# A gather of pixels on ScalarE, cut into two halves at other places of its order

## The chip, the cores and the metric

The kernel runs on one NeuronCore of a Trainium2 chip. The metric is the time of one execution on the device, in microseconds. TensorE multiplies matrices and writes to PSUM, VectorE, ScalarE and GpSimd work element by element, and SyncE starts the transfers from memory. Each engine has its own queue, is served in order, and waits on semaphores for the others.

## What is computed

128 images of 64 channels and 64 x 64 pixels go through three stages in float32. Cut to what matters:

```python
# token stage: 4 x 4 pixels of an image give one token
reduce_feats = x.mean(over the 16 pixels)                  # 256 tokens x 64 channels
q  = layernorm(reduce_feats) @ Wq.T                        # 8 heads of 8 channels
kv = layernorm(each of the 16 pixels) @ Wkv.T              # 16 keys and values a token
attn = softmax(q * scale . k over the 16 pixels)
h = reduce_feats + (attn . v) @ proj_w.T + proj_b
# linear attention with decay over the 256 tokens, in chunks of 128
scores = (q_c . k_c) * mask;  intra = scores . v_c
inter = (q_c * q_decay) . S;  S = decay * S + (k_c * k_decay) . v_c
h = layernorm(h + (intra + inter) @ w_proj + b_proj)
# eight experts, the best two for each token, weighted
h = layernorm(h + h + sum_e combine[:, e] * (gelu(h @ w1[e] + b1[e]) @ w2[e] + b2[e]))
```

(The last line has h twice, since the expert block itself returns its tokens plus the sum.)

## The kernel before

The kernel has two blocks, one behind the other. The first runs the token stage and the attention, the second the experts. The change is in the first.

**Units.** A unit is one half (128 tokens, 2048 pixels) of two images. Their 2 x 64 channels fill the 128 partitions, each with 2048 pixels in a row. There are 128 units. Every engine runs the same function `step(i, r)` for unit 4 i + r, in a loop whose body holds four units, and in each step it works at several units at once: `there(i, r, lag)` says whether the unit `lag` back exists, `done(i, r, lag, per)` gives the count that a semaphore has when that unit is done, if it is raised `per` times a unit. The order of the operations inside a step is written out by hand, for each engine apart. `s` is the unit's parity, which is also the half of the images.

**The pixels.** `xb` holds four units of pixels as they come from memory. In a row of 2048 pixels the 16 pixels of a token are four neighbours (`d`) in each of four blocks (`b`). The value product on TensorE wants them with the tokens side by side, so ScalarE copies each fourth pixel of `xb` into `xd`: `gather(j, ahead)` (L590 on, the copy at L597) brings piece d = j, all four blocks, 512 elements a partition. Pieces 0 and 1 are gathered for the next unit (`ahead` = 1) in the step before, pieces 2 and 3 in the unit's own step. Each raises `xd_done` once, four times a unit.

**ScalarE's order in a step.** gather(2); `ssb` (L606, a copy of the selected sums); gather(3); attention's queries and keys `qT`, `kT` (L615, L616), which are ready when TensorE's L447 is; squares for a layer norm (L572); `vpad` (L626), in every second unit the state copies `vpl`, `kpl` (L632, L633), and `htok` (L634), all out of TensorE's L457; centred(0) (L579); more squares; the reciprocal deviations by logarithm and exponential (L648 to L651, the last being `y0s`); centred(1); values(0) (L586, a copy of the first values); `oT` (L657); centred(2); `aggT`; gather(0) and later gather(1) of the next unit; values(1); `qqT` (L668); the exponential of the softmax (L672); centred(3).

**TensorE's order.** selected sums (L355, L359); scores of the attention (L472); its queries and keys (L446, L447); a transposition of `ssb` (L370); attention's values, keys and tokens (L457); keys 0 (L389, L394: the key product and the centred pixels for `b` = 0); queries (L431); values of pieces 0 and 1 (L416); part of attention's sums (L491); keys 1; the rest of L491; keys 2; a transposition (L507); values of pieces 2 and 3 (L416); another transposition (L440); keys 3; projections (L512, L520), and every second unit the state (L527). L457 writes the bank out of which `kT` is copied, so it waits for `qk_ev`. Ahead of it in the queue stand the waits for keys 0 (`keys_free(0)`): the pixels of the unit, the first half of the mask, and the previous unit's readers of the same banks. `values_free(v)` holds back the value products: it waits for the pieces in `xd`, by the count of `xd_done`.

**VectorE's order.** the mask (L883, two instructions, PSUM to `sm`); keys 0 (L872: key product times query, out of PSUM); the reduce of the weighted values (L894); keys 1 (L872); a Newton step on the reciprocal deviations (L901 to L903); queries; keys 2; softmax's maxima (L927 to L932); keys 3; the attention weights `aw` (L939); the token `hT` (L951) and the attention's output (L964).

**GpSimd's order.** weights times values (L711, four instructions into `pv`) as soon as `aw` is there; two sums over them (L718); `qm` (L725), `htok` (L731), `kd` or `qdm`; and the sums of the pixels (L765 to L772) for the tokens of a later unit.

Of the kernel before, what the change touches and what calls it, by code (L numbers as in the profile page):

```python
# [13 lines left out]
def vit_tower_kernel(nc, x, ln_q_w, ln_q_b, Wq, ln_kv_w, ln_kv_b, Wkv, proj_w, proj_b,  # L14
# [3 lines left out]
    ST = 4  # L18
# [18 lines left out]
    def done(i, r, lag, per, plus=0):  # L37

        if isinstance(i, int):
            return max(0, max(0, min(UNITS, 4 * i + r - lag + 1)) * per + plus)  # L40
        return i * (4 * per) + (r - lag + 1) * per + plus

    def there(i, r, lag):
        return not isinstance(i, int) or 0 <= 4 * i + r - lag < UNITS

    def pairs(i, r, back, per=1):

        if isinstance(i, int):
            return max(0, min(UNITS // 2, 2 * i + r // 2 + back)) * per
        return i * (2 * per) + (r // 2 + back) * per  # L50
# [32 lines left out]
    with ExitStack() as ctx:  # L83
# [3 lines left out]
        def sem(name):  # L87
            return ctx.enter_context(nc.semaphore(name))
# [47 lines left out]
        with ExitStack() as early:  # L136
            def sb1(name, shape, dt=F32):
                return early.enter_context(nc.sbuf_tensor(name, shape, dt))
# [19 lines left out]
            xb = sb1("xb", [P, 4, PX])  # L158
            xt = sb1("xt", [P, PX // 2])
            xd = sb1("xd", [P, ST, PX // ST])  # L160
# [50 lines left out]
            xd_done = sem("xd_done")  # L211
# [56 lines left out]
            def heads(ap):  # L268
                return ap.rearrange("p (m c) -> p m c", c=C)
# [57 lines left out]
            def _(pe):  # L327
# [16 lines left out]
                def step(i, r):  # L344
# [54 lines left out]
                    def values_free(v):  # L399

                        if there(i, r, 0):
                            pe.wait_ge(mask_done, done(i, r, 4, NM))
                            pe.wait_ge(vs_done, done(i, r, 1, NV, v))
                            pe.wait_ge(xd_done, done(i, r, 1, ST, 2 * v + 2))

                    def values(v):

# [127 lines left out]
                    attn_vk()  # L535
                    keys(0)
                    values_free(0)
                    queries()
                    values(0)
                    attend(0)  # L540
                    keys(1)
                    attend(1)
                    keys(2)
                    values_free(1)
                    aggregated()
                    values(1)
# [9 lines left out]
            def _(act):  # L556
# [9 lines left out]
                def step(i, r):  # L566
# [3 lines left out]
                    def squares(src, dst, to=None):  # L570

                        return nc.scalar.activation(src if to is None else to, src, ACT.Square, accum_out=dst)  # L572

                    def centred(j):

                        if there(i, r, 0):
                            act.wait_ge(kc_pe, done(i, r, 1, ST, j + 1))
                            act.wait_ge(sel_pe, done(i, r, 1, 1))
                            nc.scalar.activation(sqs[:, j, :], CB, ACT.Square).then_inc(cs_done, 1)  # L579

                    def values(v):

                        if there(i, r, 0):
                            act.wait_ge(v_pe, done(i, r, 1, NV, v + 1))
                            act.wait_ge(pv_ch, done(i, r, 2, ST, 2 * v + 2 - ST))
                            nc.scalar.activation(  # L586
                                vs[:, s, v * 8 * P:(v + 1) * 8 * P].rearrange("p (n m c) -> p m n c", m=2, c=C),
                                ps[:, 2:4, :].rearrange("p m (n c) -> p m n c", c=C), ACT.Copy).then_inc(vs_done, 1)

                    def gather(j, ahead):  # L590

                        if there(i, r, -ahead):
                            f = (r + ahead) % 4
                            if j == 0:
                                act.wait_ge(x_in[f], 16 * NL * (i + 1 + (r + ahead) // 4))
                            act.wait_ge(v_pe, done(i, r, 1 - ahead, NV, j // 2 + 1 - NV))
                            nc.scalar.activation(  # L597
                                xd[:, j, :].rearrange("p (b t) -> p b t", b=ST),
                                xb[:, f, :].rearrange("p (b t d) -> p d b t", b=ST, d=ST)[:, j],
                                ACT.Copy).then_inc(xd_done, 1)  # L600

                    gather(2, 0)
                    if there(i, r, 1):
                        act.wait_ge(sel_pe, done(i, r, 1, 1))
                        act.wait_ge(tr_pe, done(i, r, 2, 1))
                        nc.scalar.activation(ssb[:], B7, ACT.Copy).then_inc(sev_done, 1)  # L606
                    gather(3, 0)
                    if there(i, r, 3):
                        act.wait_ge(qk_pe, done(i, r, 3, 1))
                        act.wait_ge(sc_done, done(i, r, 5, 4))  # L610
# [6 lines left out]
                    if there(i, r, 5):  # L617

                        act.wait_ge(lt_done, done(i, r, 5, 1))
                        for m in range(2):  # L620
                            ins = squares(LT[:, m * CR:m * CR + C], ssq[:, m:m + 1], l2[:, m * C:(m + 1) * C])
                        ins.then_inc(ln_sq, 1)
                    if there(i, r, 3):
                        act.wait_ge(vk_pe, done(i, r, 3, 1))
                        act.wait_ge(lt_done, done(i, r, 5, 1))
                        nc.scalar.activation(  # L626
                            vpad[:, o, :].rearrange("p (m h w) -> p m h w", m=2, w=VW)[:, :, :, 0:D],
                            B67[:, :, 0:C].rearrange("p m (h d) -> p m h d", d=D), ACT.Copy).then_inc(vk_ev, 1)
                        if s == 1:
                            act.wait_ge(s_pe, pairs(i, r, -1))  # L630
                            act.wait_ge(kd_done, pairs(i, r, -1))
                            nc.scalar.activation(heads(vpl[:]), B67[:, :, 0:C], ACT.Copy).then_inc(st_ev, 1)  # L632
                            nc.scalar.activation(heads(kpl[:]), B67[:, :, C:2 * C], ACT.Copy).then_inc(st_ev, 1)  # L633
                        nc.scalar.activation(htok[:, o, :].rearrange("p (m c) -> p m c", c=CR),  # L634
                                             B67[:, :, 2 * C:2 * C + CR], ACT.Copy).then_inc(vk_ev, 1)
# [13 lines left out]
                    link(nc.scalar.activation(lnv[:], sgr[:, :, 16:19], ACT.Ln, bias=eps_c[:, 0:1], scale=1.0 / C))  # L649
                    link(nc.scalar.activation(y0[:], lnv[:], ACT.Exp, scale=-0.5))  # L650
                    nc.scalar.activation(y0s[:], y0[:], ACT.Square).then_inc(rs_ch, 1)  # L651
                    centred(1)
                    values(0)
                    if there(i, r, 4):
# [4 lines left out]
                    if there(i, r, 2):  # L659
                        act.wait_ge(agT_pe, done(i, r, 2, 1))  # L660
                        act.wait_ge(pj_done, done(i, r, 3, 1))
                        nc.scalar.activation(aggT[:], B6[:, 0:P], ACT.Identity, bias=bv_col[:, 0:1],
                                             scale=N / WS).then_inc(agT_ev, 1)
                    gather(0, 1)
                    values(1)
                    if there(i, r, -1):
# [7 lines left out]
                    centred(3)  # L674
                    gather(1, 1)
                units(act, step)

            @block.gpsimd
# [743 lines left out]
```

## Time and profile before

| | us |
|---|---|
| median of three runs | 2465.64 |
| lowest, highest | 2463.54, 2467.04 |
| profiled execution | 2467.91 |
| its span | 2466.0 |

| engine | busy us | share of the span | instructions |
|---|---|---|---|
| TensorE, matmuls | 2225.0 | 90% | 32433 |
| TensorE, weight loads | 1025.5 | 42% | 32433 |
| VectorE | 1830.5 | 74% | 4000 |
| ScalarE | 1844.4 | 75% | 4405 |
| GpSimd | 1883.8 | 76% | 2077 |

The span is the time from the first to the last record of one execution, taken by the hardware profiler. Busy times are sums over records; records of one engine can overlap by a little, as an instruction starts before the last one's end is recorded. PE is TensorE, PEld its weight loads, DVE VectorE, ACT ScalarE, POOL GpSimd, SP SyncE; L12 is line 12 of the kernel.

### The profile page before, as it was taken

How to read it: one execution, taken by the hardware profiler on the slowest of the kernel's cores; microseconds unless marked ns; L12 is line 12 of the kernel's file. 1: busy time of each engine (PE TensorE's matmuls, PEld its weight loads, DVE VectorE, ACT ScalarE, POOL GpSimd, SP SyncE). 2: the span in 40 equal slices, each digit the busy share in tenths (PEclk: the TensorE clock that was granted, in tenths of full speed). 3: DMA queues.
4: the chain of work that ended last, by engine and by line, in shares of the span. 5: the costliest groups of instructions: out<-in, count | busy, mean ns of one | idle time of the engine just before them, and what ended most of it. 6: DMA issues, size and time to landing. Idle time of an engine off the chain costs nothing. (4 is left out here: it accounts for less than half of the span.)

```text
span 2466.0 us, 90547 instructions
## 1 busy us (share of the span) xinstructions
PE 2225.0 (90%) x32433; PEld 1025.5 (42%) x32433; DVE 1830.5 (74%) x4000; ACT 1844.4 (75%) x4405; POOL 1883.8 (76%) x2077
## 2 busy tenths in 40 slices
PE   1799999999999999999999999999999976999997
PEld 0344444444444444444444444444444442332222
DVE  4577777777777777777777777777777766777775
ACT  1888888888888888888888888888888854555554
POOL 2788889888889989888898888888888951333333
PEclk9999999999999999999999999999999987999999
DMA  4333333333333333333333333333333200110001
GB/s 83 71 71 70 70 71 73 72 73 72 72 73 71 70 70 70 70 70 70 70 70 70 70 70 70 70 70 70 71 73 73 47 2 1 24 23 21 20 22 28
DMA packets 573782, 147.91 MB, mean 60 GB/s; under 512 B 573504, under 2 KB 573504, under 8 KB 573504
## 3 DMA queue, kind: packets, MB, share of 16 engines
q1 hardware_dynamic: 573504, 143.53, 29.1%
q8 instruction: 256, 4.19, 0.7%
q14 instruction: 22, 0.18, 0.0%
HBM read 135.10 MB, written 8.39 MB: 58 GB/s over the span
## 5 line engine op out<-in xcount | busy, mean ns | idle before, releaser
L711 POOL TENSOR_TENSOR pv<-vs,aw 128x512 f32<-128x512 f32 x512 | 535.7, 1079 | 172.5 <-DVE aw L939 172.5
L597 ACT ACTIVATE xd<-xb 128x512 f32<-128x512 f32 x512 | 589.2, 1186 | 0.0
L389 PE MATMUL ps<-xb,w_ckv 64*64 64x512 f32 x2048 | 551.4, 615 | 5.4 <-DVE kqs L872 4.3
L394 PE MATMUL ps<-xb,w_ckv 64*64 64x512 f32 x2048 | 551.4, 615 | 0.0
L872 DVE TENSOR_TENSOR kqs<-ps,qqT 128x512 f32<-128x512 f32 x512 | 353.8, 691 | 231.1 <-PE ps L394 221.3
L579 ACT ACTIVATE sqs<-ps 128x512 f32<-128x512 f32 x512 | 308.5, 603 | 239.7 <-PE ps L394 239.5
L883 DVE TENSOR_TENSOR sm<-ps,decay 128x1024 f32<-128x1024 f32 x256 | 301.5, 1219 | 149.8 <-PE ps L472 149.8
L765 POOL TENSOR_TENSOR xt<-xb 128x512 f32<-128x512 f32 x256 | 326.2, 1275 | 23.2 <-issue 22.7
L718 POOL TENSOR_TENSOR pv<-pv 128x512 f32<-128x512 f32 x256 | 320.3, 1273 | 0.0
L416 PE MATMUL ps<-w_ckv,xd 64*64 64x64 f32 x16384 | 297.8, 221 | 0.0
L416 PEld LDWEIGHTS ps<-w_ckv,xd 64*64 64x64 f32 x16384 | 262.9, 135 | 33.9 <-issue 1.8
L894 DVE TENSOR_REDUCE agg<-pv 128x128 f32<-128x1024 f32 x128 | 253.5, 1981 | 24.4 <-POOL pv L718 18.9
L586 ACT ACTIVATE vs<-ps 128x1024 f32<-128x1024 f32 x256 | 261.9, 1023 | 0.5 <-PE ps L416 0.5
L1241 ACT ACTIVATE hid<-ps,b1p 128x1024 f32<-128x1024 f32 x128 | 142.7, 1115 | 131.8 <-PE ps L1154 131.7
L1358 DVE TENSOR_TENSOR hid<-ps,hid 128x512 f32<-128x512 f32 x256 | 162.9, 685 | 87.3 <-PE ps L1166 77.7
L491 PE MATMUL ps<-sm,vpad 128*32 128x128 f32 x4096 | 192.0, 284 | 34.6 <-DVE kqs L872 30.4
L768 POOL TENSOR_TENSOR xt<-xt 128x512 f32<-128x512 f32 x128 | 163.9, 1281 | 10.0
L491 PEld LDWEIGHTS ps<-sm,vpad 128*32 128x32 f32 x4096 | 90.6, 109 | 179.7 <-issue 106.8
L1086 POOL TENSOR_TENSOR outb<-y,yrs 128x512 f32<-128x512 f32 x32 | 33.4, 1043 | 154.3 <-DVE yrs L1378 154.3
L472 PE MATMUL ps<-qm,kT 32*128 32x512 f32 x1024 | 148.8, 651 | 0.0
L457 PE MATMUL ps<-w_av,hT 64*128 64x200 f32 x512 | 78.4, 376 | 77.1 <-ACT kT L616 76.7
L355 PE MATMUL ps<-kqs,selk 128*32 128x512 f32 x1024 | 136.4, 605 | 11.7 <-DVE kqs L872 2.7
(227 smaller groups left out, 4145.5 us busy)
## 6 DMA issues: line engine op xcount, KB each, us to landing
xb<-in_x_dram SPq DMA_DIRECT2D x512, 256.0 KB, 4.3
out_dram<-outb SPq DMA_DIRECT2D x128, 64.0 KB, 1.6
w1p<-in_L_ffn_w_dram SPq DMA_DIRECT2D x16, 16.0 KB
w2p<-in_L_ffn_w_dram SPq DMA_DIRECT2D x8, 16.0 KB
b1p<-in_L_ffn_b_dram SPq DMA_DIRECT2D x8, 0.2 KB
b2v<-in_L_ffn_b_dram SPq DMA_DIRECT2D x8, 2.0 KB
sm<-in_L_tok_Wkv_dram SPq DMA_DIRECT2D x4, 16.0 KB, 2.0
w_av<-in_L_attn_w_qkv_dram SPq DMA_DIRECT2D x4, 16.0 KB, 2.1
```

The source lines that it names most:

```text
L389: nc.tensor.matmul(KB[own, :], w_ckv[own, 2 * P + m * C:2 * P + (m + 1) * C], xv[own, j], start=True, stop=True)
L394: mm = nc.tensor.matmul(CB[(1 - m) * C:(2 - m) * C, :], w_ckv[own, m * C:(m + 1) * C], xv[own, j], start=True, stop=True)
L416: mm = nc.tensor.matmul(VB[m][h * C:(h + 1) * C, n * C:(n + 1) * C], xv[own, d, b, h * C:(h + 1) * C], w_ckv[own, P + m * C:P + (m + 1) * ...
L491: mm = nc.tensor.matmul(B5[g * W:(g + 1) * W, 0:P], vpad[:, s, at:at + W], sm[:, (4 * g + jj) * P:(4 * g + jj + 1) * P], start=(jj == 0), ...
L579: nc.scalar.activation(sqs[:, j, :], CB, ACT.Square).then_inc(cs_done, 1)
L586: nc.scalar.activation(vs[:, s, v * 8 * P:(v + 1) * 8 * P].rearrange("p (n m c) -> p m n c", m=2, c=C), ps[:, 2:4, :].rearrange("p m (n c) ...
L597: nc.scalar.activation(xd[:, j, :].rearrange("p (b t) -> p b t", b=ST), xb[:, f, :].rearrange("p (b t d) -> p d b t", b=ST, d=ST)[:, j], A ...
L711: nc.gpsimd.tensor_tensor(pv[:, at].rearrange("p (k d) -> p k d", d=D), vs[:, s, at].rearrange("p (k d) -> p k d", d=D), aw[:, j * W4:(j + ...
L718: nc.gpsimd.tensor_tensor(pv[:, j * 4 * P:(j + 1) * 4 * P], pv[:, j * 4 * P:(j + 1) * 4 * P], pv[:, (j + 2) * 4 * P:(j + 3) * 4 * P], ALU. ...
L765: ins = nc.gpsimd.tensor_tensor(xt[:, h * H:(h + 1) * H], xb[:, f, h * H:(h + 1) * H], xb[:, f, (h + 2) * H:(h + 3) * H], ALU.add)
L872: V.tensor_tensor(kqs[:, j, :].rearrange("p (t d) -> p t d", d=ST), KB.rearrange("p (t d) -> p t d", d=ST), qqT[:, s, :].unsqueeze(2).to_b ...
L883: V.tensor_tensor(sm[:, f * 1024:(f + 1) * 1024].rearrange("p (h c) -> p h c", c=P), ps[:, 2 * f:2 * f + 2, :].rearrange("p g (h c) -> p ( ...
```

## The change

The gather of the fourth piece, gather(3), stood between `ssb` and `qT`. It is done in two instructions of two blocks each (256 elements a partition): the first stands behind the squares and ahead of `vpad`, the second behind `y0s` and ahead of centred(1). `xd_done` now rises five times a unit, and the counts for which TensorE waits follow: 5 per unit, 2 for the first value product, 5 for the second.

```diff
@@ TensorE
-                            pe.wait_ge(xd_done, done(i, r, 1, ST, 2 * v + 2))
+                            pe.wait_ge(xd_done, done(i, r, 1, ST + 1, 3 * v + 2))
@@ ScalarE
-                    def gather(j, ahead):
+                    def gather(j, ahead, b0=0, b1=ST):
                             nc.scalar.activation(
-                                xd[:, j, :].rearrange("p (b t) -> p b t", b=ST),
-                                xb[:, f, :].rearrange("p (b t d) -> p d b t", b=ST, d=ST)[:, j],
+                                xd[:, j, :].rearrange("p (b t) -> p b t", b=ST)[:, b0:b1],
+                                xb[:, f, :].rearrange("p (b t d) -> p d b t", b=ST, d=ST)[:, j, b0:b1],
                                 ACT.Copy).then_inc(xd_done, 1)
@@
                         nc.scalar.activation(ssb[:], B7, ACT.Copy).then_inc(sev_done, 1)
-                    gather(3, 0)
                     if there(i, r, 3):
@@
                         ins.then_inc(ln_sq, 1)
+                    gather(3, 0, 0, ST // 2)
                     if there(i, r, 3):
                         act.wait_ge(vk_pe, done(i, r, 3, 1))
@@
                     nc.scalar.activation(y0s[:], y0[:], ACT.Square).then_inc(rs_ch, 1)
+                    gather(3, 0, ST // 2, ST)
                     centred(1)
```

## Rows read from the trace of the kernel before

**Rows 1.** The page, part 1: busy us (share of the span) xinstructions.

```profile
PE 2225.0 (90%) x32433; PEld 1025.5 (42%) x32433; DVE 1830.5 (74%) x4000; ACT 1844.4 (75%) x4405; POOL 1883.8 (76%) x2077
```

**Rows 2.** Busy time by stretch: stretch, length, PE, PEld, DVE, ACT, POOL, clock, DMA.

```profile
60.00:2025.00 1965.00, 1824.08 (x30623) 896.13 (x30619) 1491.00 (x3129) 1612.25 (x4079) 1736.38 (x1903) 1.00 0.34 68
```

**Rows 3.** The line L939 alone: durations in ns, first and last start in us.

```profile
L939 DVE TENSOR_TENSOR aw<-ps,yrs x128: 414/425/426, 80.7 to 2011.6; 128x256 f32<-128x256 f32 x128
```

**Rows 4.** The waits: who waited for whom, us in total, times, longest.

```profile
PE ps L457 <- ACT kT L616: 76.7, 126, 0.9
...
DVE agg L894 <- POOL pv L718: 18.9, 82, 2.6
```

**Rows 5.** Timeline of ScalarE: start, duration, instruction, [idle before it, what ended it].

```profile
1027.80 1.20 ACT L597 ACTIVATE xd<-xb 128x512 f32<-128x512 f32 x1
1028.87 0.30 ACT L615 ACTIVATE qT<-ps 128x128 f32<-128x128 f32 x1
1029.03 0.31 ACT L616 ACTIVATE kT<-ps 128x128 f32<-128x128 f32 x1
...
1029.49 0.26 ACT L572 ACTIVATION_READ_ACCUMULATOR l<-ps 128x1 f32 x1
1030.23 0.28 ACT L626 ACTIVATE vpad<-ps 128x128 f32<-128x128 f32 x1 [0.49 <-PE ps L457]
...
1033.19 0.24 ACT L651 ACTIVATE y0s<-y 128x48 f32<-128x48 f32 x1
1034.18 0.60 ACT L579 ACTIVATE sqs<-ps 128x512 f32<-128x512 f32 x1 [0.75 <-PE ps L394]
```

**Rows 6.** Timeline of TensorE, the same unit and the one before it.

```profile
1015.80 0.50 PE L431 MATMUL ps<-w_qc,h 64*128 64x136 f32 x4
...
1028.14 0.39 PE L447 MATMUL ps<-hT,w_ak 128*128 128x128 f32 x2
...
1029.59 0.61 PE L457 MATMUL ps<-w_av,hT 64*128 64x200 f32 x4 [0.58 <-ACT kT L616]
```

**Rows 7.** Timeline of GpSimd: the two sums, in two units that follow each other.

```profile
1014.10 2.50 POOL L718 TENSOR_TENSOR pv<-pv 128x512 f32<-128x512 f32 x2
...
1029.70 2.50 POOL L718 TENSOR_TENSOR pv<-pv 128x512 f32<-128x512 f32 x2
```

**Rows 8.** Timeline of VectorE in the unit of rows 5.

```profile
1027.94 2.36 DVE L883 TENSOR_TENSOR sm<-ps,decay 128x1024 f32<-128x1024 f32 x2 [1.30 <-PE ps L472]
...
1032.32 1.96 DVE L894 TENSOR_REDUCE agg<-pv 128x128 f32<-128x1024 f32 x1 [0.19 <-POOL pv L718]
1034.21 0.67 DVE L872 TENSOR_TENSOR kqs<-ps,qqT 128x512 f32<-128x512 f32 x1
```

**Rows 9.** Timeline of VectorE in the two units before that.

```profile
1001.69 1.98 DVE L894 TENSOR_REDUCE agg<-pv 128x128 f32<-128x1024 f32 x1
1003.75 0.69 DVE L872 TENSOR_TENSOR kqs<-ps,qqT 128x512 f32<-128x512 f32 x1
...
1016.64 2.00 DVE L894 TENSOR_REDUCE agg<-pv 128x128 f32<-128x1024 f32 x1
1018.84 0.69 DVE L872 TENSOR_TENSOR kqs<-ps,qqT 128x512 f32<-128x512 f32 x1 [0.20 <-PE ps L394]
```

**Rows 10.** Timeline of TensorE near the end of the first stage.

```profile
2002.88 0.39 PE L447 MATMUL ps<-hT,w_ak 128*128 128x128 f32 x2
...
2003.80 0.61 PE L457 MATMUL ps<-w_av,hT 64*128 64x200 f32 x4
```

**Rows 11.** Timeline of ScalarE at the same place.

```profile
2003.31 0.28 ACT L615 ACTIVATE qT<-ps 128x128 f32<-128x128 f32 x1 [1.08 <-PE ps L447]
2003.48 0.27 ACT L616 ACTIVATE kT<-ps 128x128 f32<-128x128 f32 x1
```

**Rows 12.** Timeline of ScalarE in a unit with the state copies.

```profile
1015.24 0.31 ACT L634 ACTIVATE htok<-ps 128x144 f32<-128x144 f32 x1
```

**Rows 13.** Groups of instructions by form: line, operation, count, busy us, mean ns, idle before.

```profile
L597 ACT ACTIVATE xd<-xb 128x512 f32<-128x512 f32 x512 | 589.2, 1186 | 0.0
```

## The prediction

> **What bounds the kernel now.** I read the page first: TensorE is busy for nine tenths of the span [rows 1]. Then the stretches: 1965 of the 2466 us are the first stage (tokens, queries, attention), at full granted clock, and the change lies wholly in it [rows 2]. Its 128 units come at one pace: the product that makes the attention weights (L939) starts first at 80.7 and last at 2011.6 us, so (2011.6 - 80.7) / 127 = 15.20 us a unit [rows 3]. A change is worth what it takes off those 15.20 us.
>
> A busy engine does not say which wait closes the loop, so the waits come next. TensorE stops once in each unit, at L457 (attention's values, keys and tokens), for ScalarE's copy of the keys: 76.7 us in 126 stops, 0.61 us each [rows 4]. And VectorE's reduce of the weighted values (L894) waits for GpSimd in 82 units. These are two different loops through the same unit, and the forecast hangs on how close the second is to the first.
>
> *Loop B, over TensorE.* In the unit shown, ScalarE runs the gather of the fourth piece from 1027.80; only then come qT at 1028.87 and kT at 1029.03, ending at 1029.34 [rows 5]. TensorE's key product L447 had ended at 1028.14 + 0.39 = 1028.53. L457 starts at 1029.59, 0.25 us after kT's end [rows 6]. Behind it stand in order the first key product, the queries, the values, and the second key product, which VectorE multiplies at 1034.21 (L872).
>
> *Loop A, over GpSimd.* aw -> four products and two sums on GpSimd, the last ending at 1029.70 + 2.50 = 1032.20 [rows 7] -> L894 at 1032.32 -> L872 on the second key product at 1034.21, 1.89 us after L894's start, with no idle time before it [rows 8] -> the third and fourth keys -> the next aw. This loop holds no instruction that the change touches.
>
> Which loop ends last at that L872 is read from its distance to L894. Where GpSimd's loop binds it is 1.89. In a neighbouring unit it is 1003.75 - 1001.69 = 2.06, and in the one between 1018.84 - 1016.64 = 2.20, there with 0.20 us of idle time that TensorE's L394 ends [rows 9]. The pattern follows the loop of four units: two of four read 2.2, one 2.06, one 1.89, and it repeats through the stage. So loop A could close earlier than now by 0.31, 0.17, 0.31 and 0 us: 0.79 over four units, 0.20 a unit.
>
> **The change, part by part.**
>
> *Taken away ahead of qT.* One gather, start to next start 1028.87 - 1027.80 = 1.07 us. qT then waits for L447 instead. At the stage's end, where no gather runs, the trace shows that case: L447 ends at 2002.88 + 0.39 = 2003.27 and qT starts 0.04 later [rows 10, 11]. So qT would start at 1028.57, 0.30 us earlier, not 1.07: ScalarE would idle for the rest. kT ends at 1029.04.
>
> *What is late next at L457.* Its queue of waits has also the first half of the mask (L883 writes sm out of the banks that the keys need): two instructions from 1027.94 for 2.36 us, so the first ends near 1029.13 [rows 8]. The bounds of the lag behind it are 0.05 us (kT's end 2003.75 to L457 at 2003.80) [rows 10, 11] and the 0.25 us of now. L457 therefore goes to between 1029.29 (kT plus 0.25) and 1029.38 (mask plus 0.25): 0.21 to 0.30 us earlier. I take 0.28, as the lag of a wait that is met early is nearer to 0.05.
>
> *First half of the gather, ahead of vpad.* It stands behind the squares, whose last record starts at 1029.49, so after the shift at 1029.19, and begins about 0.14 later (ScalarE records overlap by that much: 1.20 of duration against 1.07 of spacing) [rows 5]. Price: half of 1.07 plus half of the fixed part. The fixed part is at least nothing and at most the 0.16 us that a 128-element copy takes in all (1028.87 to 1029.03), so 0.54 to 0.62 us; as an outer bound the whole 1.07. Vpad can start at 1029.33 + 0.54 to 0.62 = 1029.87 to 1029.95. It needs L457, which then ends at 1029.59 + 0.61 - 0.28 = 1029.92. So it is covered by the 0.49 us of idle time now ahead of vpad, with next to nothing over. Queued behind it are vpad, in every second unit the two state copies, and htok; TensorE's queries (L431) wait for these, at 1015.80 after htok's end at 1015.24 + 0.31 = 1015.55 [rows 6, 12].
>
> *Second half, ahead of centred(1).* Behind y0s at 1033.19 ScalarE idles 0.75 us for TensorE [rows 5]. Shifted with loop B by 0.28, a half from about 1033.06 frees ScalarE at 1033.60 to 1033.68, and the second square is due at 1034.18 - 0.28 = 1033.90. Nothing is charged. VectorE's reciprocal chain waits for y0s, which is ahead of it. TensorE's second value pass, the reader of the fourth piece, comes over 2 us later; its count of five gathers a unit instead of four adds no wait, and the first pass asks for the two pieces gathered in the unit before, as now. Nothing is issued to the DMA queues by it.
>
> A whole gather of 512 elements takes 1186 ns in the mean [rows 13]. The Trainium skill, VectorE: DVE Perf Modes, "The TRN2 errata", says that ScalarE operations with a source in SBUF pay a fixed latency in every instruction, 224 cycles at 1.2 GHz, so that cutting one in two is a loss of 0.19 us a unit; charged in full on the path this would be 24 us over the stage and undo the gain. No row here prices a half, but both halves stand in idle time (0.49 and 0.75 us), so by this rule too the sum stays as it is. The Trainium skill, Advanced Engine Details and Errata, "SBUF Cachelines", charges an access for every new 16-byte line; this gather takes one float of each, which would make its cost go with the elements and a half cost half.
>
> **The sum.** Per unit the gain is the smaller of B's 0.28 and A's room: 0.28, 0.17, 0.28, 0, together 0.73 in four units, 0.18 a unit, and 22.6 us over 124 units in steady state. One thing takes from it: where GpSimd truly binds, L894 starts 0.12 us after the last sum (1032.20 to 1032.32), in the other kinds 0.04 (1014.10 + 2.50 to 1016.64) [rows 7 to 9]. If these take on the 0.08 that lie between, the four units gain 0.23, 0.09, 0.23 and 0, and 5.6 us go; I let about half of it go: 20 us. Profiled execution: 2467.9 (span 2466.0 and 1.9 around it) - 20 = 2447.9. It lies 2.3 us above the median of the three runs, so the forecast for the median is 2465.6 - 20 = 2445.6 us; its own range, with 0.21 to 0.30 at L457 (18 to 24 us) and all or none of the 0.08, is 2442 to 2453.
>
> **The rivals.**
>
> *Both loops shorten (2431 us).* If loop A's 1.89 us is not a floor, every unit gains 0.28: 34.7 us. Against it: GpSimd's durations and the reduce are not touched.
>
> *The second half disturbs the reduce (2454 us).* ScalarE would read SBUF while L894 reads it, from 1033.06 on, which it doesn't now. With 0.1 us more on L894 the rooms are 0.21, 0.07, 0.21 and -0.1: 0.39 in four, 12 us. No row shows such an overlap with a reduce.
>
> *L457 gets no earlier (2464 us, no change).* The change would then move qT and nothing behind it: were the mask or another of the waits already as late as kT, nothing but scheduling noise would be left. For it: the stop at L457 ends 0.25 us after kT, five times the 0.05 us of the stage's end. Against: several waits stand in that queue, and the difference fits their being worked off one by one.
>
> *A half costs like a whole (2476 us, slower).* One place: ahead of vpad. The half would end at 1029.33 + 1.07 = 1030.40, 0.17 us after vpad's start now (1030.23). In every second unit, where the state copies follow, L431 waits 0.25 us behind htok [rows 6, 12], and TensorE is 0.17 us later than now: 64 x 0.17 = 11 us more. It decides from a half of 0.90 us on.
>
> **How the numbers follow.** Forecast 0.57; reduce disturbed 0.10; both loops 0.08; no earlier 0.12; half like whole 0.13. Anything within 0.2% (4.9 us) can't be told from no change here. Faster: 0.57 + 0.10 + 0.08, less 0.02 for the edge, 0.73; same 0.14; slower 0.13. For the range 0.08 (both loops) is left out below and most of the slower rival above: 2434 to 2466.
>
> **What the profile of the changed kernel would show.** qT 0.04 us behind L447 with idle time ahead of it; the stop at L457 cut from 0.61 to about 0.33 us; halves of 0.6 to 0.75 us each, starting 0.5 to 0.6 us before their successor can; idle time ahead of vpad near nothing and ahead of the second square 0.2 to 0.3; L894's wait for GpSimd in nearly all units and more in sum; 1.9 us from L894 to the next L872 nearly everywhere; the pace of L939 at about 15.04 us. Wrong it would be by a half of over 0.9 us, a longer L894, or an L457 that stays put.

## The result, and the profile after

The changed kernel takes 2450.2 us (median, 2448.9 to 2452.2) against 2466.3 for the kernel before (2463.5 to 2467.9) in the same runs: a ratio of 0.9934 with a 95% interval of 0.9919 to 0.9948. The gain is 16.1 us where 20 were forecast; the time is 4.6 us above the forecast of 2445.6 and inside its range of 2434 to 2466. The profiled execution took 2449.9 us with a span of 2448.0, 18.0 less than before.

The page's part 1, the stretch of the first stage and the line of the attention weights (now L940; the lines behind the edit have moved by one) answer to [rows 1 to 3]. Their columns are the same.

```profile
PE 2225.4 (91%) x32433; PEld 1025.9 (42%) x32433; DVE 1825.7 (75%) x4000; ACT 1859.5 (76%) x4533; POOL 1884.4 (77%) x2077
```

```profile
60.00:2010.00 1950.00, 1826.33 (x30625) 897.64 (x30623) 1488.19 (x3131) 1627.70 (x4212) 1737.14 (x1904) 1.00 0.34 69
```

```profile
L940 DVE TENSOR_TENSOR aw<-ps,yrs x128: 414/424/426, 80.6 to 1994.4; 128x256 f32<-128x256 f32 x128
```

ScalarE has 128 instructions and 15 us of work more, TensorE's granted clock is the same 1.00 in this stage, and the kernel is faster. The pace is (1994.4 - 80.6) / 127 = 15.07 us a unit, 0.13 less than before [rows 3], and 127 of these are 17 of the 18 us. So all but about 1 us of the gain is made in the loop of the first stage, as the forecast had it.

The waits say what closes the loop now (engine, line, waited for: us in total, times, longest), to be read against [rows 4]:

```profile
ACT qT L614 <- PE ps L447: 103.8, 127, 4.5
...
DVE agg L895 <- POOL pv L719: 47.4, 127, 2.6
...
PE ps L457 <- ACT kT L615: 30.4, 60, 0.6
PE ps L457 <- DVE sm L884: 23.2, 66, 0.5
...
ACT vpad L626 <- PE ps L457: 2.1, 5, 0.7
```

TensorE's stop at L457 fell from 76.7 to 53.6 us, and 66 of its 126 stops are now put down to the mask. VectorE's wait for GpSimd rose from 18.9 us in 82 units to 47.4 in 127. ScalarE's idle time ahead of vpad is gone, since the first half fills it; in the kernel before it was:

```profile
ACT vpad L626 <- PE ps L457: 63.6, 128, 0.9
```

Timelines of the changed kernel show the mechanism and the part of it that was not foreseen. First ScalarE's, with four units that follow each other, in the numbering of the table below the units 1, 2, 3 and 0 of the round (start, duration, instruction, idle time before it and what ended it):

```profile
1005.48 0.28 ACT L614 ACTIVATE qT<-ps 128x128 f32<-128x128 f32 x1 [0.60 <-PE ps L447]
...
1006.21 0.70 ACT L597 ACTIVATE xd<-xb 128x256 f32<-128x256 f32 x1
1006.84 0.28 ACT L626 ACTIVATE vpad<-ps 128x128 f32<-128x128 f32 x1
...
1020.98 0.28 ACT L614 ACTIVATE qT<-ps 128x128 f32<-128x128 f32 x1 [0.90 <-PE ps L447]
...
1035.82 0.28 ACT L614 ACTIVATE qT<-ps 128x128 f32<-128x128 f32 x1 [0.76 <-PE ps L447]
...
1051.18 0.28 ACT L614 ACTIVATE qT<-ps 128x128 f32<-128x128 f32 x1 [0.81 <-PE ps L447]
```

Then TensorE's in the same four units:

```profile
1005.06 0.39 PE L447 MATMUL ps<-hT,w_ak 128*128 128x128 f32 x2
1006.19 0.61 PE L457 MATMUL ps<-w_av,hT 64*128 64x200 f32 x4 [0.27 <-DVE sm L884]
...
1020.27 0.39 PE L447 MATMUL ps<-hT,w_ak 128*128 128x128 f32 x2
1021.67 0.61 PE L457 MATMUL ps<-w_av,hT 64*128 64x200 f32 x4 [0.54 <-ACT kT L615]
...
1035.24 0.39 PE L447 MATMUL ps<-hT,w_ak 128*128 128x128 f32 x2
1036.52 0.61 PE L457 MATMUL ps<-w_av,hT 64*128 64x200 f32 x4 [0.41 <-DVE sm L884]
...
1050.55 0.39 PE L447 MATMUL ps<-hT,w_ak 128*128 128x128 f32 x2
1051.88 0.61 PE L457 MATMUL ps<-w_av,hT 64*128 64x200 f32 x4 [0.47 <-ACT kT L615]
```

From L447's end to qT's start it is 0.03 us (1005.06 + 0.39 to 1005.48), then 0.32, 0.19 and 0.24. The key product is there in all four units; what differs is the queue of waits ahead of qT. The source writes them in the same order for every unit, but the compiled program does not keep it. The records of the waits themselves, which the grouped views leave out, have the key product's first and three or four others behind it in units 0, 2 and 3; in unit 1 the others stand ahead of it, done by 1003.9, and the key product's is the last. L457 follows: its stop is 0.27 us in the unit with the short lag and 0.54 in the one with the long lag, where next to nothing is left of the gain (0.58 in [rows 6]).

The mask's first half, by which L457 also waits, takes 1.22 us of the 2.36 (VectorE, in units 1 and 3):

```profile
1004.87 2.36 DVE L884 TENSOR_TENSOR sm<-ps,decay 128x1024 f32<-128x1024 f32 x2 [1.09 <-PE ps L472]
...
1035.05 2.35 DVE L884 TENSOR_TENSOR sm<-ps,decay 128x1024 f32<-128x1024 f32 x2 [0.90 <-PE ps L472]
```

In unit 1 it ends at 1006.09, 0.10 us ahead of L457, and kT 0.26 ahead. In unit 3 it ends at 1036.27 together with kT, so this view's choice between the two says little; L457 starts 0.25 us behind kT's end there, as it does in units 0 and 2 and in the kernel before.

VectorE's timeline shows the other loop closing (units 1, 2 and 3), L895 to the second L873, to be read against [rows 8, 9]:

```profile
1009.08 1.99 DVE L895 TENSOR_REDUCE agg<-pv 128x128 f32<-128x1024 f32 x1 [0.50 <-POOL pv L719]
1010.98 0.68 DVE L873 TENSOR_TENSOR kqs<-ps,qqT 128x512 f32<-128x512 f32 x1
...
1024.44 2.01 DVE L895 TENSOR_REDUCE agg<-pv 128x128 f32<-128x1024 f32 x1 [0.22 <-POOL pv L719]
1026.37 0.68 DVE L873 TENSOR_TENSOR kqs<-ps,qqT 128x512 f32<-128x512 f32 x1
...
1039.26 1.98 DVE L895 TENSOR_REDUCE agg<-pv 128x128 f32<-128x1024 f32 x1 [0.35 <-POOL pv L719]
1041.25 0.69 DVE L873 TENSOR_TENSOR kqs<-ps,qqT 128x512 f32<-128x512 f32 x1
```

1.90, 1.93 and 1.99 us, where before the same kinds of unit had 2.20, 1.89 and 2.19 (the table has the last). GpSimd's loop now closes three of the four units. In the fourth, unit 3, the table has 2.08 against 1.92 in the others, so 0.16 us of room is left there.

To compare kernels unit by unit, a table was made from each trace: for the units 24 to 103 (20 rounds of the loop), sorted by their place in the round, the mean distance between two starts of `aw`, the median lag from L447 to qT, and the median distance from the reduce to the key product behind it. Unit 0 is the kind read as 2.06 in the forecast, unit 1 the 2.20, unit 2 the 1.89, unit 3 the second of those at 2.2. Differences given in the text are taken before rounding.

| kernel | distance of `aw`, units 0 to 3 | mean | L447 to qT | reduce to key product |
|---|---|---|---|---|
| before | 14.95, 15.52, 15.06, 15.44 | 15.243 | 0.34 to 0.36 in all | 2.05, 2.20, 1.90, 2.19 |
| after | 14.82, 15.23, 15.07, 15.28 | 15.101 | 0.25, 0.04, 0.32, 0.19 | 1.92, 1.92, 1.92, 2.08 |
| e1, one wait ahead of qT | 14.79, 15.24, 15.07, 15.16 | 15.068 | 0.04 in all | 1.90, 1.93, 1.93, 1.93 |
| e2, GpSimd's waits | 14.82, 15.19, 14.98, 15.26 | 15.063 | as after | 2.00, 1.95, 2.08, 1.99 |
| e5, all waits | 14.73, 15.14, 14.82, 15.14 | 14.957 | 0.04 in all | 1.93, 1.91, 1.91, 1.92 |

### The profile page after: what moved, and what is told of

Read it like the earlier page. It is cut to its first block and busy times, and to the rows that moved or that the text cites. A ratio compares the mean times of both kernels' runs of the same rounds, so it can differ in the third digit from the quotient of the medians.

```text
span 2448.0 us, 90675 instructions
## 1 busy us (share of the span) xinstructions
PE 2225.4 (91%) x32433; PEld 1025.9 (42%) x32433; DVE 1825.7 (75%) x4000; ACT 1859.5 (76%) x4533; POOL 1884.4 (77%) x2077
## 5 line engine op out<-in xcount | busy, mean ns | idle before, releaser
L597 ACT ACTIVATE xd<-xb 128x512 f32<-128x512 f32 (+1 forms) x640 | 608.8, 979 | 0.0
L873 DVE TENSOR_TENSOR kqs<-ps,qqT 128x512 f32<-128x512 f32 x512 | 353.3, 690 | 195.4 <-PE ps L394 185.7
L895 DVE TENSOR_REDUCE agg<-pv 128x128 f32<-128x1024 f32 x128 | 255.3, 1994 | 47.5 <-POOL pv L719 47.4
L1155 PE MATMUL ps<-tokT,w1p 64*128 64x512 f32 x512 | 145.9, 648 | 0.0
```

Source lines behind the costliest of these rows:

```text
L597: nc.scalar.activation(xd[:, j, :].rearrange("p (b t) -> p b t", b=ST)[:, b0:b1], xb[:, f, :].rearrange("p (b t d) -> p d b t", b=ST, d=ST ...
L873: V.tensor_tensor(kqs[:, j, :].rearrange("p (t d) -> p t d", d=ST), KB.rearrange("p (t d) -> p t d", d=ST), qqT[:, s, :].unsqueeze(2).to_b ...
```

## The experiments

The theory (1) is that two loops run through every unit, TensorE's over L457 and GpSimd's over the weighted values, and the later one closes it; the change shortened the first by up to 0.3 us until the second stood in the way, and gave away some of that to the waits ahead of qT. The rivals are (2) that TensorE's loop alone sets the pace, and (3) that what was short of the forecast is the price of the two halves.

**e1: one wait ahead of qT.** This is the changed kernel without the other waits ahead of qT (four, in every second unit three), which earlier waits of the same engine already make sure of.

```diff
                         act.wait_ge(qk_pe, done(i, r, 3, 1))
-                        act.wait_ge(sc_done, done(i, r, 5, 4))
-                        act.wait_ge(qm_done, done(i, r, 5, 1))
-                        act.wait_ge(o_done, done(i, r, 5, 1))
-                        if s == 0:
-                            act.wait_ge(qd_done, pairs(i, r, -2))
```

> The changed kernel, but qT waits for the key product alone; the four other waits ahead of it say what earlier waits of the same queue have already made sure of. Two loops alternate (theory 1: TensorE's over L457, GpSimd's over the weighted values): qT starts 0.04 us behind L447 in all four units of the loop (now 0.04, 0.19, 0.25 and 0.32), L457 comes up to 0.25 us earlier, but GpSimd's loop closes in three of four units, so only about 5 us are gained: 2445 us. Theory 2 (TensorE's loop alone sets the pace): 0.16 us a unit, 20 us: 2430 us. Theory 3 (what was short of the forecast is the price of the halves on ScalarE): no gain, 2450 us.

Measured: 2448.6 us (2447.5 to 2449.2), ratio 0.9925 (0.9912 to 0.9939). Against the changed kernel's 2450.2 the medians differ by 1.6 us and the intervals overlap; in the table the pace falls by 0.033 us a unit, and from the first to the last `aw` it is 3.0 us less (81.3 to 1992.2 us). That is less than the 5 us of theory 1, and by the medians alone it could be nothing, as theory 3 has it; it is e4 that decides on theory 3. Its two timelines, ScalarE and TensorE, in one unit and the next:

```profile
1004.97 0.28 ACT L609 ACTIVATE qT<-ps 128x128 f32<-128x128 f32 x1 [0.62 <-PE ps L447]
...
1020.18 0.28 ACT L609 ACTIVATE qT<-ps 128x128 f32<-128x128 f32 x1 [0.60 <-PE ps L447]
```

```profile
1004.54 0.39 PE L447 MATMUL ps<-hT,w_ak 128*128 128x128 f32 x2
1005.67 0.61 PE L457 MATMUL ps<-w_av,hT 64*128 64x200 f32 x4 [0.27 <-DVE sm L879]
1019.75 0.39 PE L447 MATMUL ps<-hT,w_ak 128*128 128x128 f32 x2
1020.88 0.61 PE L457 MATMUL ps<-w_av,hT 64*128 64x200 f32 x4 [0.27 <-DVE sm L879]
```

The lag is 0.04 us in every unit and L457's stop 0.27 in all of them, so the lags of 0.19 to 0.32 were those waits and nothing else. L457 comes 0.16 to 0.26 us earlier behind L447 in three of four units, and yet only unit 3 got much faster, by 0.13 (unit 0 by 0.03): it was the one with 2.08 us between reduce and key product. Theory 2 wanted 20 us.

**e2: GpSimd's loop shortened.** This is the changed kernel, where on GpSimd and VectorE the wait that is met last stands alone.

```diff
@@ GpSimd
-                        pool.wait_ge(aw_done, done(i, r, 2, 1))
-                        pool.wait_ge(agg_ch, done(i, r, 3, 1))
-                        pool.wait_ge(vs_done, done(i, r, 2, NV))
+                        if not there(i, r, -1):
+                            pool.wait_ge(vs_done, done(i, r, 2, NV))
+                        pool.wait_ge(aw_done, done(i, r, 2, 1))
@@ GpSimd, ahead of the last instruction of the step before
+                        pool.wait_ge(vs_done, done(i, r, 1, NV))
                         pool.wait_ge(qp_pe, done(i, r, -1, 1))
@@ VectorE
                         dve.wait_ge(pv_done, done(i, r, 2, 2))
-                        dve.wait_ge(agg_done, done(i, r, 3, 1))
```

> The changed kernel, but GpSimd's first product waits for the attention weights alone (its other waits moved ahead of the instruction before, or dropped as already made sure of), and VectorE's reduce for the sums alone. GpSimd's loop gets 0.08 to 0.17 us shorter. Theory 1 (two loops alternate): the units in which it closes the loop gain up to the distance to TensorE's, 0.1, 0.06, 0 and 0 us of four, about 5 us: 2445 us. Theory 2 (TensorE's loop alone): no change, 2450 us. A theory in which GpSimd's loop alone sets the pace: 0.13 us a unit, 16 us: 2434 us.

Measured: 2445.1 us (2443.5 to 2447.0), ratio 0.9913 (0.9900 to 0.9927), as theory 1 had it in sum: 0.15 us in four units against 0.16. Its spread was another: 0.01, 0.04, 0.08 and 0.02 us in units 0 to 3, where two units were to have 0.1 and 0.06 and the others nothing. More than half of the gain is in unit 2, the unit that gained nothing by the change itself. The weights' product and GpSimd's first product in two units, VectorE first:

```profile
1000.72 0.42 DVE L940 TENSOR_TENSOR aw<-ps,yrs 128x256 f32<-128x256 f32 x1
1015.89 0.42 DVE L940 TENSOR_TENSOR aw<-ps,yrs 128x256 f32<-128x256 f32 x1
```

```profile
1001.22 4.18 POOL L712 TENSOR_TENSOR pv<-vs,aw 128x512 f32<-128x512 f32 x4 [0.63 <-DVE aw L940]
1016.40 4.19 POOL L712 TENSOR_TENSOR pv<-vs,aw 128x512 f32<-128x512 f32 x4 [1.04 <-DVE aw L940]
```

It is 0.50 us from the start of the one to that of the other in all units (0.50 to 0.67 before and after, by the place in the round). So GpSimd's loop does set the pace in some units of the changed kernel: theory 2 alone falls.

**e3: the whole gather ahead of vpad.** In the changed kernel both halves become one instruction at the place of the first, and TensorE counts four gathers a unit, as before.

```diff
-                    gather(3, 0, 0, ST // 2)
+                    gather(3, 0)
@@
-                    gather(3, 0, ST // 2, ST)
```

> The changed kernel, but the whole fourth gather stands ahead of vpad. This is the place of the slower rival: vpad 0.45 us later than in the changed kernel, htok too, and the queries on TensorE 0.43 us later in every second unit and 0.24 us in the others, 0.27 us a unit after the slack of the loop: 2483 us. If the place ahead of vpad is not on the path: 2450 us.

Measured: 2479.0 us (2478.3 to 2482.1), ratio 1.0053 (1.0037 to 1.0068): slower than before the change. ScalarE and then TensorE, in a unit with the state copies:

```profile
1020.78 1.18 ACT L597 ACTIVATE xd<-xb 128x512 f32<-128x512 f32 x1
1021.84 0.30 ACT L626 ACTIVATE vpad<-ps 128x128 f32<-128x128 f32 x1
```

```profile
1022.90 0.50 PE L431 MATMUL ps<-w_qc,h 64*128 64x136 f32 x4 [0.47 <-ACT htok L634]
```

The queries stop for `htok`, as the slower rival said they would, and the time is near the 2476 us that it gave. In the mean of its units vpad starts 0.45 us behind L457's end instead of 0.04. So the rival's mechanism is real; what did not hold is its condition, a half that costs like a whole.

**e4: no fourth gather.** It is left out of the changed kernel, and the piece stays zero (one memset more in the set-up); TensorE counts three gathers a unit.

```diff
+                link(V.memset(xd[:], 0.0))
@@
-                    gather(3, 0, 0, ST // 2)
@@
-                    gather(3, 0, ST // 2, ST)
```

> The changed kernel without the gather of the fourth piece: it is left out, the piece is zero throughout. Theories 1 and 2 (the halves lie in idle time): 2449 us, as the changed kernel. Theory 3 (the halves are paid for on the path, in ScalarE's time or in the reduce that runs beside the second): 2440 us or less.

Measured: 2453.8 us (2452.1 to 2454.7), ratio 0.9946 (0.9931 to 0.9962). Not faster than the changed kernel, but 3.6 us slower; of these 2.8 are the memset: the first `aw` starts at 83.3 instead of 80.6 us. The pace by the table's method is 15.095 us against 15.101. So the halves cost about 0.006 us a unit, under 1 us together, and theory 3 falls. What can be seen of them is in the reduce, in the groups of e4 first and of the changed kernel second (mean ns behind the busy time):

```profile
L894 DVE TENSOR_REDUCE agg<-pv 128x128 f32<-128x1024 f32 x128 | 253.1, 1978 | 47.8 <-POOL pv L717 47.6
```

```profile
L895 DVE TENSOR_REDUCE agg<-pv 128x128 f32<-128x1024 f32 x128 | 255.3, 1994 | 47.5 <-POOL pv L719 47.4
```

**e5: all waits.** e1 and e2 together, and on TensorE:

```diff
@@ keys_free
                             if j == 0:
-                                pe.wait_ge(x_in[r], 16 * NL * (i + 1))
                                 pe.wait_ge(mask_done, done(i, r, 4, NM, 1 - NM))
+                                return
@@ attn_vk
                             pe.wait_ge(qk_ev, done(i, r, 3, 2))
-                            pe.wait_ge(sev_done, done(i, r, 1, 1))
@@ ahead of attn_qk()
+                    if there(i, r, 0):
+                        pe.wait_ge(x_in[r], 16 * NL * (i + 1))
```

> The changed kernel with the edits of e1 and e2 together, and on TensorE L457 waits for the copies and the mask alone (the pixels' wait moved ahead of the attention's queries, the others dropped as already made sure of). Theory 1 (two loops alternate): the reduce-to-key-product distances of e2 (2.00, 1.95, 2.08, 1.99 us) leave 0.08, 0.03, 0.16 and 0.07 us to GpSimd's floor of 1.92, 0.085 a unit, 10 us below e2: 2435 us, with 1.9 us in all four units. Theory 2 (TensorE's loop alone): its own gain is 0.19 us a unit, 24 us: 2421 us.

Measured: 2433.4 us (2432.4 to 2434.6), ratio 0.9867 (0.9852 to 0.9882): 12 us below e2 and 17 below the changed kernel, the fastest of all. The edits of e1 and e2 gave 1.6 and 5.1 us alone; together with the third they give 16.8, which is what two loops in turn do: each edit alone runs into the other loop. The third edit, on TensorE, was not run alone, nor the first two without it. It takes 0.05 us off the stop at L457 (0.27 to 0.22), and if all of that were gained in every unit it would be 6 us; the 11 that are left are still more than the sum of 6.7. The waits of e5:

```profile
DVE agg L891 <- POOL pv L715: 61.8, 127, 2.7
...
PE ps L456 <- DVE sm L881: 27.9, 124, 0.3
```

TensorE stops 0.22 us at this place, in nearly all units for the mask; the reduce is followed by the key product at 1.91 to 1.93 us in all four units, GpSimd's floor.

**e6: the kernel before with e2's edit.** The first lines of it:

```diff
@@ GpSimd
-                        pool.wait_ge(aw_done, done(i, r, 2, 1))
-                        pool.wait_ge(agg_ch, done(i, r, 3, 1))
-                        pool.wait_ge(vs_done, done(i, r, 2, NV))
+                        pool.wait_ge(aw_done, done(i, r, 2, 1))
...
@@ VectorE
-                        dve.wait_ge(agg_done, done(i, r, 3, 1))
```

> The kernel before with e2's edit alone. Theory 1: GpSimd closes the loop there in one unit of four, by 0.03 us: 1 us, 2465 us, no change. If GpSimd's loop sets the pace of the kernel before as well: 0.13 us a unit, 16 us, 2450 us.

Measured: 2463.7 us (2462.9 to 2467.6), ratio 0.9995 (0.9986 to 1.0004): no change. Before the change GpSimd's loop had room in three of four units, and shortening it gave nothing. In the fourth, unit 2, the two loops end together: with the edit the distance from reduce to key product rises from 1.90 to 2.13 us, and the unit gets no faster (15.05 us against 15.06). Behind the change the same edit gave 5 us.

**e7: the whole gather ahead of centred(1).** In the changed kernel both halves become one instruction at the place of the second, with four gathers a unit again.

```diff
-                    gather(3, 0, 0, ST // 2)
@@
-                    gather(3, 0, ST // 2, ST)
+                    gather(3, 0)
```

> The changed kernel, but the whole fourth gather stands ahead of centred(1), behind the reciprocal deviations. It takes 1.07 us of an idle stretch of 0.75: the second square is 0.14 to 0.23 us late and holds TensorE by 0.03 to 0.1 us a unit: 2458 us. If the squares have slack enough: 2450 us, and cutting the gather in two was not needed.

Measured: 2467.7 us (2465.2 to 2469.7), ratio 1.0006 (0.9996 to 1.0015). The expectation had the place right and the price too small by 10 us. ScalarE, then TensorE:

```profile
1003.69 1.17 ACT L597 ACTIVATE xd<-xb 128x512 f32<-128x512 f32 x1
1004.75 0.59 ACT L579 ACTIVATE sqs<-ps 128x512 f32<-128x512 f32 x1
```

```profile
1005.49 0.42 PE L491 MATMUL ps<-sm,vpad 128*32 128x128 f32 x8 [0.44 <-ACT sqs L579]
```

The second square comes right behind the gather and ends at 1005.34; TensorE stops for it 0.44 us, where it stopped 0.24 for VectorE in the changed kernel. From the key product to the next `aw` it is 0.09 to 0.19 us more than in the changed kernel. This stretch belongs to both loops, so nothing absorbs a delay in it. The whole gather fits neither of the two places; that is why the cut pays.

**e8: the kernel before with e1's edit.** The same waits are dropped, in the kernel before.

```diff
                         act.wait_ge(qk_pe, done(i, r, 3, 1))
-                        act.wait_ge(sc_done, done(i, r, 5, 4))
-                        act.wait_ge(qm_done, done(i, r, 5, 1))
-                        act.wait_ge(o_done, done(i, r, 5, 1))
-                        if s == 0:
-                            act.wait_ge(qd_done, pairs(i, r, -2))
```

> The kernel before with e1's edit alone: qT waits for the key product alone. Theory 1: the queue of waits lies under the fourth gather there, so nothing changes: 2466 us. If the waits cost time of ScalarE wherever they stand: 5 us or more less.

Measured: 2467.0 us (2463.4 to 2469.8), ratio 1.0001 (0.9992 to 1.0011): nothing. The lag from L447 to qT stays at 0.34 to 0.35 us in all units. The same queue of waits was there before, but was worked off while the fourth gather ran. The change took this cover away.

## Why the prediction was right, and where it was off

*What bounds the kernel*: right. Loop B over L457 and loop A over GpSimd are what e1, e2, e5 and e6 show, and the floor of 1.89 us between reduce and key product holds: no kind of unit is below 1.90 in any run of the table, and those that GpSimd's loop closes have 1.90 to 1.93.

*qT earlier by 0.30 us*: right for one unit of four. The trace of the stage's end, on which the 0.04 us rested [rows 10, 11], shows a unit whose other waits stand ahead of the key product's in the compiled program and were done 1.5 us before it. In three units of the loop the key product's wait stands first, and the others, though met, are worked off behind it. So the step failed for the units 0, 2 and 3, with 0.25, 0.32 and 0.19 us. The prediction named such waits, worked off one by one, for L457 and did not ask for them at qT. The gains by unit show it: forecast 0.17, 0.28, 0 and 0.28, measured 0.12, 0.29, -0.01 and 0.16 (the table's first two rows). That is 0.57 us a round instead of 0.73, or 17.7 instead of 22.6 us over 31 rounds, and 3.7 of the 4.9 us that are short are unit 3's, the one in which TensorE's loop is the later. The rest is mostly unit 0's, where the room was 0.13 (2.05 to the 1.92 of now) and not 0.17.

*The mask as next at L457*: right in unit 1, and in e1 in 124 units, at 0.27 us against the 0.33 forecast. L457 is then 0.10 us behind the mask's first half, not the 0.25 that was the bound. In the other units kT is as late or later. Counted from L447's end, L457 comes 0.12, 0.34, 0.06 and 0.18 us earlier in units 0 to 3, where 0.28 was forecast for all.

*The room of loop A*: right, and the term that decided the size. The lags of 0.04 and 0.12 us behind the last sum stayed as they were (0.03 and 0.12 by the table's method), so the deduction of 2.6 us for them was not needed; it happened to cover half of the other miss, which is why 20 us came so near. That part was luck.

*The first half ahead of vpad*: right. A half takes 683 ns by its record. Vpad starts 0.63 us after the half's start, and in all four kinds of unit 0.04 us behind L457's end, as in the kernel before. So it is still L457 that lets vpad go; the half's price is 0.62 us at most (0.54 to 0.62 forecast), and it is covered with next to nothing over. e3 shows what comes of more.

```profile
L597 ACT ACTIVATE xd<-xb 128x512 f32<-128x512 f32 x384 | 434.0, 1175 | 0.0
...
L597 ACT ACTIVATE xd<-xb 128x256 f32<-128x256 f32 x256 | 174.9, 683 | 0.0
```

*The second half ahead of centred(1)*: right, nothing to be paid; e7 shows that the idle time there would not have borne the whole. The reduce beside it grew from 1978 to 1994 ns, a sixth of the 0.1 us that the rival had supposed, and e4 leaves under 1 us for it and the halves together.

*The rivals.* Both loops shorter: no, unit 2 gained nothing. L457 no earlier: nearly true of unit 2 (0.06 us), though not for this rival's reason: the mask ended 0.38 us ahead of L457 there, and what was late was kT, behind the waits ahead of qT. A half like a whole: no, 0.58 of a whole by the records.

## What to carry to other kernels

Work that stands ahead of a late wait can also be the cover under which a queue of other waits is worked off. When it is moved away, drop the waits that an earlier wait of the same engine has made sure of, move others ahead, or see to it that the one met last is the last of the queue. No run only changed the order; that it would do is read from unit 1. The order to look at is that of the compiled program: here it differed between units that have the same source. Where two loops run through a stage, read at the place where they meet how far the second is behind the first: it is the most that shortening the first can bring, and for more than that the two must be shortened together.

## What the runs showed of the hardware

A wait that is already met is not free when it stands behind one that is met late. With three or four more of them behind it, qT started 0.19, 0.25 and 0.32 us behind its data instead of 0.04 (after and e1); with the others moved or dropped, GpSimd's first product started up to 0.17 us earlier behind the weights, and VectorE's reduce in unit 2 0.09 us earlier behind the sum (e2).

A gather of every fourth float costs ScalarE 1175 ns for 512 elements and 683 for 256, so by these records 1.92 ns an element and 2 x 683 - 1175 = 191 ns for each instruction, while ScalarE's squares from PSUM, 512 elements side by side, take 602. The 191 ns agree with the fixed 224 cycles at 1.2 GHz (187 ns) that the Trainium skill, VectorE: DVE Perf Modes, "The TRN2 errata", gives for a source in SBUF; there was idle time to hold them. The same row has one cycle an element (0.83 ns) besides, and there the measurement of this strided gather differs: 1.92 ns.
